# One program for two transformer blocks: written-out engine orders for the feed-forward and the final FFN

## What is computed

```python
x = x + cross_block(layernorm(x), cond, ctx)
x = x + ffn(layernorm(x))
```

```python
u = h3 @ ff_w1 + ff_b1            # 256 -> 2 x 1024
a, gate = split(u, 2)
y = a * gelu(gate) @ ff_w2 + ff_b2 + x
```

```python
def bitlinear(x, w, b):
    r = rmsnorm(x)                               # x * rsqrt(mean(x*x) + 1e-5)
    s = 127 / max(max(abs(r)), 1e-5)             # per token
    xq = clip(round(r * s), -128, 127) / s
    t = 1 / max(mean(abs(w)), 1e-5)
    wq = clip(round(w * t), -1, 1) / t
    return xq @ wq.T + b
ffn = bitlinear(gelu(bitlinear(x, w1, b1)), w2, b2)
```

## The kernel before

| In the profile | In the code |
|---|---|
| scores<-hT,weights L924 | up |
| outs<-weights,attn_outT L940 | down |
| mixed<-identf,normed L769 | normT |
| mixed<-identf,attn_outT L955 | front_T |
| L967 / L976 | tern_T / mm1 |
| L985 / L993 | gelu_T / mm2 |
| L1753, L1747, L1760 | gated, z_low, residual |
| L1802 to L1815 | front_quantise |
| L1825, L1831, L1837 to L1844, L1848 | linear, gelu_max, gelu_columns, gelu_quantise |
| L1483, L1522 and L1524 | add_x, mean_power |

## Time and profile before

### The profile page before, as it was taken

One profiled execution on the slowest core, in us unless ns is written; L12 is line 12 of the kernel. 1 busy time (PEld: TensorE's weight loads), 2 busy tenths in 40 slices (PEclk: granted clock), 3 DMA queues, 4 the chain that ended last, 5 costly groups with the idle time before them and its releaser, 6 DMA issues.

```text
span 1269.9 us, 30602 instructions
## 1 busy us (share of the span) xinstructions
PE 1130.8 (89%) x12732; PEld 736.7 (58%) x12739; DVE 867.5 (68%) x1724; ACT 593.1 (47%) x855; POOL 681.1 (54%) x602
## 2 busy tenths in 40 slices
PE   4789999999999999999999998988999799799776
PEld 1245655665665665655665665666666566365554
DVE  5667767756756667757757658578679666765764
ACT  3335454444344344444444455444445442465555
POOL 5657866755655666757755654356346443511230
PEclk7799999999999999999999999999999999999987
DMA  7230220220220220220220222234333520000001
GB/s 270 58 109 2 51 51 2 52 51 7 46 51 9 45 51 3 51 51 2 52 51 2 51 51 68 43 67 121 82 64 74 162 76 1 1 5 14 17 1 34
DMA packets 41855, 63.52 MB, mean 50 GB/s; under 512 B 11460, under 2 KB 22384, under 8 KB 41462
## 3 DMA queue, kind: packets, MB, share of 16 engines
q1 hardware_dynamic: 40413, 60.91, 19.1%
q10 hardware_dynamic: 1304, 0.66, 0.2%
HBM read 20.63 MB, written 2.10 MB: 18 GB/s over the span
## 4 chain that ended last, share of the span: by engine, by line
PE 61%; DVE 17%; DMA 7%; ACT 6%; issue 6%; SPq 2%; POOL 1%; ACTq 0%; DVEq 0%
PE outs L806 9%; PE scores L865 7%; PE scores L866 7%; PE mixed L827 6%; DMA head_operands<-neg_max_rows 5%; PE outs L783 4%; PE scores L924 4%; PE outs L890 3%; PE outs L888 3%; PE outs L889 3%; PE outs L940 3%; DVE maxes L1670 3%; DVE exps_rest L1693 2%; PE outs L816 2%; SPq L673 2%
## 5 line engine op out<-in xcount | busy, mean ns | idle before, releaser
L1459 POOL TENSOR_TENSOR exps_rest<-exps 128x1024 f16<-128x1024 f32 (+1 forms) x297 | 511.5, 1730 | 317.3 <-ACT exps L1169 316.5
L1169 ACT ACTIVATE exps<-scores 128x1024 f32<-128x1024 f32 (+1 forms) x320 | 296.8, 936 | 281.3 <-PE scores L866 251.7
L1670 DVE TENSOR_REDUCE maxes<-mixed 128x1 f32<-128x512 f32 x512 | 334.3, 684 | 81.1 <-PE mixed L827 77.6
L865 PE MATMUL scores<-head_operands 128*128 128x512 f16 (+1 forms) x576 | 219.8, 382 | 24.3 <-DMA head_operands<-neg_max_rows 23.7
L888 PE MATMUL outs<-values,exps 128*128 128x65 f16 (+1 forms) x2176 | 226.6, 193 | 1.2 <-POOL exps_rest L1459 1.2
L889 PE MATMUL outs<-values,exps 128*128 128x64 f16 (+1 forms) x2176 | 226.6, 192 | 0.0
L890 PE MATMUL outs<-values,exps_rest 128*128 128x65 f16 (+1 forms) x2176 | 226.4, 194 | 0.0
L866 PE MATMUL scores<-head_operands 128*128 128x512 f16 (+1 forms) x576 | 219.6, 381 | 0.0
L889 PEld LDWEIGHTS outs<-values,exps 128*128 128x128 bf16 (+1 forms) x2176 | 200.5, 98 | 24.8 <-issue 0.2
L888 PEld LDWEIGHTS outs<-values,exps 128*128 128x128 bf16 (+1 forms) x2176 | 201.6, 98 | 22.7 <-POOL exps_rest L1459 2.2
L890 PEld LDWEIGHTS outs<-values,exps_rest 128*128 128x128 f16 (+1 forms) x2176 | 200.4, 97 | 0.0
(11 more groups left out here) (200 smaller groups left out, 1599.7 us busy)
## 6 DMA issues: line engine op xcount, KB each, us to landing
head_operands<-qk_pairs SPq DMA_DIRECT2D x128, 256.0 KB, 4.2
head_operands<-qk_pairs SPq DMA_DIRECT2D x32, 128.0 KB, 2.4
stage<-in_L_xcond_ff_w_dram SPq DMA_DIRECT2D x3, 1024.0 KB, 5.6
residual<-in_x_dram SPq DMA_DIRECT2D x4, 512.0 KB, 9.7
stage<-in_L_ffn_w_dram SPq DMA_DIRECT2D x2, 1024.0 KB, 5.1
head_operands<-in_x_dram SPq DMA_DIRECT2D x1, 2048.0 KB, 10.2
out_dram<-out_tile SPq DMA_DIRECT2D x16, 128.0 KB, 1.7
attn_outT<-in_L_xcond_attn_wq_dram SPq DMA_DIRECT2D x1, 1024.0 KB, 8.2
```

What stands on the lines that cost most here:

```text
L865: mm(o, kb[:, KH, :], hb[:, QS, :], start=True, stop=False)
L1169: A(E[0:a.ks, c % RING, 0:n], SP_[c % 2][0:a.ks, 0:n], ACT.Exp, scale=SCALE).then_inc(s.exps, 1)
L1459: G.tensor_tensor(R[0:a.ks, c % RING, 0:n], e, e.bitcast(BF16).rearrange("p (n two) -> p n two", two=2)[:, :, 1], ALU.subtract).then_inc(s ...
L1670: V.tensor_reduce(mx[:, h, t, kh:kh + 1], m[:, :], AX_X, ALU.max).then_inc(s.maxed, 1)
```

## The change

In the stretch from chunk 1 to the end, the loops are replaced by written-out lists, one for each of TensorE, ScalarE, GpSimd and VectorE, and every entry of TensorE's list names the semaphore that frees its bank. Thirteen of the sixteen first-layer tiles go to the score banks (all but tiles 1, 4 and 9). The multiplier for rounding is computed on VectorE in two steps from the maximum, 1 / (max(amax, FLOOR) / 127) with FLOOR = 1e-5 times the root of 1e-5, where five steps went over the reciprocal root; the scale that `linear` and `finish` need is computed on GpSimd by `front_scale` and `gelu_scale`, three small steps each. Chunk 0, attention and all DMAs are unchanged. The lists of ScalarE are cut here.

```diff
 MAGIC = 1.5 * 2.0 ** 23
+FLOOR = 1e-5 * EPS ** 0.5
...
         q1_rr, q2_sq, q2_ms, q2_rr = sem("q1_rr"), sem("q2_sq"), sem("q2_ms"), sem("q2_rr")
+        q1_step, q1_scale, q2_step, q2_scale = sem("q1_step"), sem("q1_scale"), sem("q2_step"), sem("q2_scale")
...
-            return MM[:, :] if i < 2 * TPH else SP_[i % 2][:, :]
+            return SP_[i % 2][:, :] if i in (0, 2, 3, 5, 6, 7, 8, 10, 11, 12, 13, 14, 15) else MM[:, :]
...
-            def up(tc, f):
-                at_least(pe, z_full, tc * FC + f - 1)
+            def up(tc, f, *free):
+                for bank_free in free:
+                    pe.wait_ge(*bank_free)
+                if f == 0 and tc > 1:
+                    pe.wait_ge(hT_done, 2 * NT + (tc + 1) * TPH)
...
-            def down(tc, t):
-
-                if tc == 0 and t < 2:
-                    pe.wait_ge(x_new, 2 * 2 * NT - 1 + t)
-                if tc and t < 2:
-                    at_least(pe, out_ready, tc * TPH + t - 5)
-                if t > 1 or tc < 2:
-                    pe.wait_ge(y_done, CREDIT + tc * TPH + t - 1)
+            def down(tc, t, *free):
+
+                for bank_free in free:
+                    pe.wait_ge(*bank_free)
+                if t == 0:
+                    pe.wait_ge(z_lo, (tc + 1) * FC)
...
+                up(0, f, *([(z_full, f - 1)] if f > 1 else []))
+                steps(0, f)
+
+            up(1, 0, (z_full, 7))
+            up(1, 1, (z_full, 8))
+            steps(1, 0)
+            pe.wait_ge(split_done, 11)
+            down(0, 0, (x_new, 63))
+            down(0, 1, (x_new, 64))
+            steps(1, 1)
+            down(0, 2, (y_done, CREDIT + 1))
+            steps(1, 2)
+            down(0, 3, (y_done, CREDIT + 2))
+            means()
+            up(1, 2, (z_full, 9))
+            up(1, 3, (z_full, 10))
+            up(1, 4, (z_full, 11))
+            up(1, 5, (z_full, 12))
+            up(1, 6, (z_full, 13))
+            tern_T(0, (w_mean, 1))
+            up(1, 7, (z_full, 14))
+            up(2, 0, (z_full, 15))
+            front_T(0, (w_copied, 2))
+            up(2, 1, (z_full, 16))
+            down(1, 0, (y_done, CREDIT + 3))
+            mm1(0, (z_full, 17))
+            mm1(1, (q1.copied, 2))
+            down(1, 1, (y_done, CREDIT + 4))
+            mm1(2, (h_lin, 1))
+            down(1, 2, (y_done, CREDIT + 5))
+            down(1, 3, (y_done, CREDIT + 6))
+            mm1(3, (z_full, 18))
+            tern_T(1, (h_lin, 2))
+            up(2, 2, (h_lin, 3))
+            gelu_T(0, (w_copied, 4))
+            steps(1, 3)
+            up(2, 3, (h_lin, 4))
+            gelu_T(1, (q2.copied, 1))
+            mm2(0, (y_done, CREDIT + 7))
+            up(2, 4, (z_full, 19))
+            gelu_T(2, (q2.copied, 2))
+            mm2(1, (y_done, CREDIT + 8))
+            up(2, 5, (z_full, 20))
+            gelu_T(3, (q2.copied, 3))
+            up(2, 6, (z_full, 21))
+            mm2(2, (out_ready, 1))
+            up(2, 7, (z_full, 22))
+            mm2(3, (out_ready, 2))
+            up(3, 0, (z_full, 23))
+            up(3, 1, (z_full, 24))
+            front_T(1, (q2.copied, 4))
+            down(2, 0, (out_ready, 3))
+            mm1(4, (q1.copied, 4))
+            mm1(5, (z_full, 26))
+            mm1(6, (z_full, 25))
+            down(2, 1, (out_ready, 4))
+            down(2, 2, (y_done, CREDIT + 9))
+            mm1(7, (h_lin, 6))
+            down(2, 3, (y_done, CREDIT + 10))
+            up(3, 2, (h_lin, 7))
+            gelu_T(4, (h_lin, 5))
+            up(3, 3, (h_lin, 8))
+            mm2(4, (y_done, CREDIT + 11))
+            gelu_T(5, (q2.copied, 5))
+            up(3, 4, (z_full, 27))
+            gelu_T(6, (q2.copied, 6))
+            up(3, 5, (z_full, 28))
+            mm2(5, (y_done, CREDIT + 12))
+            up(3, 6, (z_full, 29))
+            gelu_T(7, (q2.copied, 7))
+            up(3, 7, (z_full, 30))
             front_T(2, (q2.copied, 8))
-            mm1(8, (z_full, NCH * FC - 1))
-            mm1(9, (z_full, NCH * FC))
-            pe.wait_ge(z_lo, NCH * FC)
-            down(3, 0)
-            down(3, 1)
+            mm2(6, (out_ready, 5))
+            mm2(7, (out_ready, 6))
+            mm1(8, (z_full, 31))
+            mm1(9, (q1.copied, 6))
+            down(3, 0, (out_ready, 7))
+            down(3, 1, (out_ready, 8))
+            down(3, 2, (y_done, CREDIT + 13))
             mm1(10, (h_lin, 9))
-            down(3, 2)
-            mm1(11, (h_lin, 10))
-            down(3, 3)
-            gelu_T(8, (q1.copied, 3 * KC))
...
+            gelu_T(8, (h_lin, 10))
             gelu_T(9, (q2.copied, 9))
             mm2(8, (y_done, CREDIT + 15))
             front_T(3, (q2.copied, 10))
-            gelu_T(10, (q1.copied, 4 * KC))
+            mm1(12, (h_lin, 11))
+            gelu_T(10, (q1.copied, 8))
+            mm1(13, (h_lin, 12))
             mm2(9, (y_done, CREDIT + 16))
-            mm1(12, (h_lin, 11))
-            mm1(13, (h_lin, 12))
             gelu_T(11, (q2.copied, 11))
-            mm2(10, (out_ready, 9))
             front_T(4, (q2.copied, 12))
-            mm2(11, (out_ready, 10))
             mm1(14, (h_lin, 13))
             mm1(15, (h_lin, 14))
-            gelu_T(12, (q1.copied, 5 * KC))
+            mm2(10, (out_ready, 9))
+            gelu_T(12, (q1.copied, 10))
+            mm2(11, (out_ready, 10))
...
             def gelu_quantise(i):
-                act.wait_ge(q2.small, 5 * (i // 2) + 5)
+                act.wait_ge(q2.small, 2 * (i // 2) + 2)
+                act.wait_ge(q2_sq, i + 1)
                 A(hbuf(i), hbuf(i), ACT.Identity, scale=gc[:, M62, i:i + 1],
                   bias=magic[:, :]).then_inc(gelu_quant_odd, 1)
...
+            steps(1, 1)
+            hi(1, 2)
+            gate(1, 3)
+            hi(1, 3)
+            gate(1, 4)
+            hi(1, 4)
+            gate(1, 5)
+            front_u(0)
+            gate(1, 6)
+            hi(1, 5)
+            hi(1, 6)
             tern_copy(0)
...
+            def front_scale(g):
+                t0, n = FRONT[g]
+                c = slice(t0, t0 + n)
+                pool.wait_ge(q1_rr, g + 1)
+                pool.wait_ge(q1.amax, g + 1)
...
+                G.tensor_tensor(fc[:, C4, c], fc[:, AM, c], fc[:, RR, c], ALU.mult).then_inc(q1_step, 1)
+                pool.wait_ge(q1_step, 2 * g + 1)
+                G.tensor_scalar(fc[:, DQ, c], fc[:, C4, c], 1e-5, 1.0 / 127.0, ALU.max, ALU.mult).then_inc(q1_step, 1)
+                pool.wait_ge(q1_step, 2 * g + 2)
+                G.tensor_tensor(fc[:, C7, c], fc[:, DQ, c], aw[:, 0, 1:2].to_broadcast([P, n]),
...
+            def gelu_scale(j):
+                c = slice(2 * j, 2 * j + 2)
+                pool.wait_ge(q2_rr, j + 1)
+                pool.wait_ge(q2.amax, j + 1)
+                G.tensor_tensor(gc[:, C42, c], gc[:, AM2, c], gc[:, RR2, c], ALU.mult).then_inc(q2_step, 1)
+                pool.wait_ge(q2_step, 2 * j + 1)
+                G.tensor_scalar(gc[:, DQ2, c], gc[:, C42, c], 1e-5, 1.0 / 127.0, ALU.max, ALU.mult).then_inc(q2_step, 1)
+                pool.wait_ge(q2_step, 2 * j + 2)
+                G.tensor_tensor(gc[:, C72, c], gc[:, DQ2, c], aw[:, 1, 1:2].to_broadcast([P, 2]),
+                                ALU.mult).then_inc(q2_scale, 1)
...
+
+            steps(1, 0)
+            steps(1, 1)
+            steps(1, 2)
+            add_x(8)
+            add_x(9)
             front(0)
+            front_scale(0)
+            add_x(10)
+            mean_power(0)
+            add_x(11)
             add_bias(0)
...
+            gelu_scale(0)
+            mean_power(1)
+            front(1)
+            steps(1, 3)
+            gelu_scale(1)
+            front_scale(1)
+            add_bias(1)
+            add_x(12)
+            mean_power(2)
+            gelu_scale(2)
+            mean_power(3)
+            add_x(13)
+            add_x(14)
+            front(2)
+            gelu_scale(3)
+            add_x(15)
+            front_scale(2)
+            add_bias(2)
             mean_power(4)
             front(3)
+            gelu_scale(4)
+            front_scale(3)
             front(4)
+            front_scale(4)
             mean_power(5)
+            gelu_scale(5)
+            mean_power(6)
             add_bias(3)
+            gelu_scale(6)
+            mean_power(7)
+            gelu_scale(7)
             add_bias(4)
-            mean_power(6)
...
                 V.tensor_reduce(fc[:, AM, c], u, AX_X, ALU.max, apply_absolute_value=True).then_inc(q1.amax, 1)
-                dve.wait_ge(q1_rr, g + 1)
                 dve.wait_ge(q1.amax, g + 1)
-                V.tensor_tensor(fc[:, C4, c], fc[:, AM, c], fc[:, RR, c], ALU.mult).then_inc(q1.small, 1)
-                dve.wait_ge(q1.small, 5 * g + 1)
-                V.tensor_scalar(fc[:, DQ, c], fc[:, C4, c], 1e-5, 1.0 / 127.0, ALU.max, ALU.mult).then_inc(q1.small, 1)
-                dve.wait_ge(q1.small, 5 * g + 2)
```

(145 more changed lines are left out.)

299 lines of the change are left out of this document (118 added, 181 removed).

## The result

The changed kernel took 1232.08 us in the median (1228.97 to 1235.71, 4 runs) where the kernel before took 1272.76 (1270.73 to 1281.41, 4 runs) beside it: a ratio of 0.9664, 95% interval 0.9637 to 0.9691. About 41 us are won; I had forecast 31. Its profiled execution took 1229.98 us with a span of 1228.2, against 1271.72 with 1269.9. The feed-forward part began 1.4 us earlier by chance (over all profiles up(1, 1) starts between 1060.9 and 1073.9 us, after an attention part that no kernel here changes), so I compare stretches, cut at the same work as in the earlier trace rows.

The account below looks back on a forecast made before the run. No engine was full; TensorE's waits and slow clock made up 57.3 us. Gains of 8.0 + 8.1 + 11.2 + 1.7 + 6.3 = 35.3, less 4 for handovers, left 31 us: 1243 us, range 1234 to 1250 (0.62).

Parts of the forecast that it names:

- A to D: Four stretches from up(1, 1) in chunk 1 to gelu_T(8), after the last down(); reordering was to remove TensorE's waits there.
- the allowance for handovers: Deduction for semaphore delays the walk ignores: eight handovers with under 1 us to spare, 0.5 us each, 4 us.
- the clock term of E: Deduction of 3.4 us in the tail: TensorE's pieces on the path take up to twice as long at clock 0.77.
- E: The tail, gelu_T(8) to the end: 35.6 us at full clock instead of 45.35; 6.3 won after the clock deduction.
- more than the walk: Rival, chance 0.06: no handover slips and the tail keeps its clock; 40 to 46 us won, 1228 to 1234.
- the walk: Following each engine's new list with traced durations, each entry starting at the later of its engine and its semaphores.
- A: The rest of chunk 1, 39.53 us before; 8.0 us to be won, with up(2, 0) starting at 1093.5 to 1094.
- B: Chunk 2: 43.6 us instead of 51.69, 8.1 won, as front_T(0)'s wait and the slow matmuls behind it go.
- C: Chunk 3: 41.1 us instead of 52.35, 11.2 won, as the waits before front_T(1) and front_T(2) go.
- D: From chunk 3 to the last down(): 16.8 us instead of 18.53, 1.7 won.
- GpSimd at no cost: Power and three small steps per group, 7.8 us, on GpSimd beside its 49 busy us of 207, costed at nothing.
- queues that block each other: Rival, chance 0.20: GpSimd's single queue blocks, and GpSimd and VectorE slow each other; 17 us won, 1257.

Follow-up runs that it names:

- e4: Changed kernel with first-layer tiles 0, 2, 3, 5, 6, 7 back in the mixed bank; A to D 141.7 us, ratio to before 0.9746.
- e5: Changed kernel with front_quantise(0), (1) and (2) moved back behind the gates on VectorE; A to D 146.9 us, ratio to before 0.9771.
- e6: Changed kernel with all eight add_x ahead of front(0) on GpSimd; A to D 136.9 us, ratio to before 0.9725.
- e7: Kernel before with 26 unread dummy matmuls ahead of gelu_T(10), (12) and (14); E 41.4 us at clock 0.96, ratio to before 0.9961.
- e11: Changed kernel with ten unread dummy matmuls ahead of mm1(12) and mm1(14); E 32.5 us at clock 1.00, ratio to before 0.9635, again 0.9700.
- e1: Changed kernel's new order with the old five-step multiplier and its wait for GpSimd's power; E 44.4 us, ratio to before 0.9752.
- c0: Control: another series of the unaltered changed kernel; 1234.18 us, ratio to before 0.9681, E 34.3 us.
- e14: Changed kernel with three idle small steps added per group on VectorE, no added wait; A to D 137.3, E 36.05 us, ratio to before 0.9761.

## Why the prediction fell short

The mechanism was right in A to D and the total too small: 31 us forecast, 40.3 in the stretches and 41.7 with the earlier start. Two steps of the sum failed, the allowance for handovers and the clock term of E; in E the split between order and multiplier was wrong as well. What came is nearest to the rival "more than the walk" (40 to 46 won, 1228 to 1234, with a chance of 0.06): of eight handovers one slipped by 0.75 and one by 0.36 us, and the tail's clock rose from 0.77 to 0.90 though it did not keep 1.00.

- **A to D, the walk.** 29.0 forecast before the allowance; 29.4 by the windows. A 9.0 for 8.0 (up(2, 0) followed after 30.52 us, where I had 31 to 31.5), B 8.3 for 8.1, C 10.2 for 11.2 (z_low's 0.75 and front_T(2)'s 0.36), D 1.9 for 1.7. That the sum agrees to 0.4 is partly luck, since A and C miss by 1.0 each in opposite directions. The reasons hold: e4, e5 and e6 brought back the waits that the prediction named, with 9.0, 14.2 and 4.2 us.
- **The allowance of 4 us failed.** It was eight handovers at 0.5 us; what slipped is the two idles of 0.75 and 0.36 us, both in C, 1.1 us, and it stands already in C's result. Against the walk's sum for A to D nothing was lost.
- **E, the clock, failed in size and in sign.** I took 3.4 us off for the low clock of the rows (0.77). But this clock was already in before's 45.35: e7 shows 4.0 us of it. The 27.0 us in the sum, called "at the full clock", were before's 29.9 at the low clock less 2.8, so the term was counted twice. The changed kernel has 0.90 and loses 2.0 (34.5 against 32.5). The change of clock gave 2 us where I deducted 3.4; this is the largest error, 5.4.
- **E, the walk.** 35.6 at the full clock, 32.5 measured in e11. From gelu_T(8) to linear(12) it was 9.0 for 8.6; the rest took 25.5 with the low clock, for 27.0. 9.7 us were forecast from before's 45.35, and at equal high clock 8.9 were won: the sum was nearly right, its parts were not. I had given 6.8 to the order, 2.8 to the steps. By the table the order alone gives 0.5, the steps alone 3.5, and 4.9 come only from both. The prediction had said that the mean and power "leave that path too", but priced them at the 0.9 us of their duration. What they held was longer: the odd tile's square on ScalarE stands before them (the idle of 2.40 us in e1), and five steps, two of them at 0.65 to 0.68 us, behind.
- **GpSimd at no cost: nearly.** Its 60 busy us of 167 leave room, and neither VectorE nor ScalarE waits for a scale step from up(1, 1) on. But the scale steps wait in its list, and what is queued behind them then falls beside VectorE's rounding: front_scale(1) and the 0.75 us in front of down(2, 0), which make most of C's miss. That is the rival "queues that block each other" in small.
- **The Trainium skill** (TensorE: Matmul & The Clock Gate, Part 4) has it that transposes do not count as TensorE's work for the clock; by it the tail would have stayed low. In e11 the clock is 1.00 over all of E, and in the changed kernel gelu_T(12) to the end, transposes and second-layer tiles in turn with idles up to 1.11 us, runs at 1.00 too (window below). e5 and e6 stay at 1.00 over all of E without any dummies. So the trace is against reading the rule as a forecast for a tail of this mix; the weight that I gave it, none in the sum, was right, and the 3.4 that I did deduct was not.

```profile
1217.00:1228.00 11.00, 6.61 (x56) 5.21 (x53) 4.02 (x9) 6.06 (x8) 3.18 (x7) 1.00 0.18 60
```

Open: what the five steps cost in the new order at one clock is split into 5.5 for the wait and 2.9 for the number (40.9 less 38.0) with the clock at 0.96 in one and 0.99 in the other. What holds the clock at 1.00 in the tails of e5 and e6, and why the attention part ends up to 13 us apart from run to run, was not looked into.

## What to carry to other kernels

Follow each engine's written list by hand with the durations of the trace: here such a walk met the 29 us won in A to D within half a us (single stretches within 1.0), and needed no allowance. When an operation is taken off a path, price not its duration alone but everything that its semaphore made wait, the other tile's work on the other engine included. And when waits become shorter, the clock they cost can come back; take the low clock out of the time before, not only out of the forecast, and compare at equal clock before saying which of two edits pays.

## What the runs showed of the chip

- TensorE's lower level came behind idles of 1.20, 1.02 and 1.20 us in a row in c0 (to 1202.86 us), where eight transposes then took 1.70 us, but not behind the same three idles in e4 (to 1213.76 us), where they took 1.04. With ten dummy matmuls of 0.22 us in the idles the clock was 1.00 and 0.99 over the 32.5 us of the tail (e11 and its repeat), 2 us less than at 0.90. In the kernel before, 26 won 4.0.
- A small step of VectorE on 128x2 took 0.17 us alone and 0.65 to 0.68 us while GpSimd was adding 128x256 rows (e1, 1215.45 and 1216.16 us), and four roundings of 128x256 took 1.14 us alone and up to 2.9 beside such additions (e14). The Trainium skill (SBUF — State Buffer, SBUF: two separate sides) has the port that the two share locked for a whole instruction; the trace agrees: the two additions in e1 run from 1215.38 to 1216.78 us, and each step ends within 0.1 us of the end of one of them.
- Stretches bound by TensorE repeat to 0.03 us between executions, while whole runs of the changed kernel vary by 10.6 us (1228.97 to 1239.55 over its three series).
